# Swin attention before an LIF layer: score products in four 64x64 tiles, q and k moved straight into their stacks

## What is computed

```
part = windows(_gn(x))                       # 8*16 windows, 64 tokens, 256 channels
q, k, v = part @ qkv_w.T + qkv_b             # q scaled by 16 ** -0.5, 16 heads
attn = einsum('wihd,wjhd->whij', q, k) + bias[None, None] + MASK[None, :, None]
attn = softmax(attn, axis=-1)
x = x + einsum('whij,wjhd->wihd', attn, v)
h = einsum('tbld,hd->tblh', _gn(x), W) + b   # then v += (h - v)/2; s = v >= 1; v = v*(1-s)
x = x + spikes
```

## Time and profile before

| | before |
|---|---|
| time, median of 3 runs | 511.57 us (507.66 to 513.79) |
| the profiled execution's own time | 516.01 us |
| its span | 514.3 us |
| granted clock of PE, mean | 0.95 |
| PE, PEld busy | 433.2 us (84%), 400.7 us (78%) |
| DVE, ACT, POOL busy | 408.8 us (79%), 380.1 us (74%), 274.8 us (53%) |
| DMA | 136780 packets, 61.56 MB, of them 107506 under 512 B |

### The profile page before, as it was taken

How to read it: one execution, slowest core, us unless ns; L and a number is a source line. 1 busy time by engine, 2 the same in 40 slices (tenths; PEclk the granted TensorE clock), 3 DMA queues, 4 the chain that set the end, 5 groups by cost and what they waited for, 6 DMA issues and landing times.

```text
span 514.3 us, 19277 instructions
## 1 busy us (share of the span) xinstructions
PE 433.2 (84%) x7848; PEld 400.7 (78%) x7848; DVE 408.8 (79%) x872; ACT 380.1 (74%) x897; POOL 274.8 (53%) x380
## 2 busy tenths in 40 slices
PE   0477956998889879889988898989898987799996
PEld 0366856987889879789878797978798986588885
DVE  7957866798789859868888778879767887588887
ACT  6357776887889869779878787978788957745560
POOL 3534674567566746567666557556756648420000
PEclk9977977999999989989999989999999989889999
DMA  7145551465555563565555555554545450023333
GB/s 216 70 104 144 126 123 47 101 149 134 126 123 136 125 151 83 144 151 130 111 147 127 135 135 132 130 135 104 112 104 116 107 138 13 22 103 124 143 128 139
DMA packets 136780, 61.56 MB, mean 120 GB/s; under 512 B 107506, under 2 KB 125172, under 8 KB 136692
## 3 DMA queue, kind: packets, MB, share of 16 engines
q1 hardware_dynamic: 136352, 60.33, 46.5%
q10 hardware_dynamic: 340, 0.01, 0.0%
HBM read 35.13 MB, written 25.17 MB: 117 GB/s over the span
## 4 chain that ended last, share of the span: by engine, by line
PE 31%; SPq 19%; ACT 13%; DMA 11%; DVE 10%; issue 7%; POOL 7%; ACTq 0%; DVEq 0%; POOLq 0%
SPq L314 13%; DMA k_stack<-k_spill0lo 5%; SPq L309 4%; PE pv_ps L1045 3%; POOL p_lo L446 3%; PE score_ps L923 3%; ACT v_hi L520 3%; PE proj_ps L923 3%; PE pv_ps L923 3%; DMA k_stack<-k_spill1lo 2%; PE proj_ps L934 2%; PE score_ps L1021 2%; ACT k_flat L503 2%; PE max_ps L923 2%; PE proj_ps L935 2%
## 5 line engine op out<-in xcount | busy, mean ns | idle before, releaser
L446 POOL TENSOR_TENSOR p_lo<-probs,p_hi 128x512 f16<-128x512 f32 x128 | 146.4, 1165 | 132.7 <-ACT p_hi L609 78.9
L1011 PE MATMUL score_ps<-q_stack,k_stack 96*128 96x64 f16 x1024 | 86.6, 194 | 45.2 <-ACT max_rows L599 18.0
L1011 PEld LDWEIGHTS score_ps<-q_stack,k_stack 96*128 96x128 f16 x1024 | 71.9, 98 | 52.5 <-ACT max_rows L599 38.5
L608 ACT ACTIVATE probs<-score_ps 128x512 f32<-128x512 f32 x128 | 77.0, 602 | 46.9 <-PE score_ps L1021 43.4
L783 DVE TENSOR_REDUCE neg_max<-max_ps 128x16 f16<-128x1024 f32 x64 | 78.3, 1224 | 27.6 <-PE max_ps L991 26.6
L934 PE MATMUL proj_ps<-xn_hi,w_hi 128*128 128x256 f32 x256 | 78.6, 307 | 12.7 <-DVE w_lo L732 8.1
L1007 PE MATMUL score_ps<-both_parts,bias_k 128*128 128x64 f16 x1024 | 78.3, 194 | 0.0
L609 ACT ACTIVATE p_hi<-score_ps 128x512 f16<-128x512 f32 x128 | 77.4, 605 | 0.0
L777 DVE TENSOR_TENSOR v_lo<-proj_ps,v_hi 64x256 f16<-64x256 f32 x128 | 54.2, 424 | 28.4 <-ACT v_hi L520 26.8
L935 PE MATMUL proj_ps<-xn_lo,w_hi 128*128 128x256 f32 x256 | 74.1, 289 | 0.0
L936 PE MATMUL proj_ps<-xn_hi,w_lo 128*128 128x256 f32 x256 | 73.8, 288 | 0.0
(11 more groups left out here) (130 smaller groups left out, 1214.2 us busy)
## 6 DMA issues: line engine op xcount, KB each, us to landing
xc<-in_x_dram SPq DMA_DIRECT2D x32, 256.0 KB, 3.5
q_spill<-q_flat SPq DMA_DIRECT2D x32, 256.0 KB, 2.7
q_stack<-q_spill SPq DMA_DIRECT2D x32, 256.0 KB, 3.7
out_dram<-xc SPq DMA_DIRECT2D x32, 256.0 KB, 2.3
q_stack<-q_spill SPq DMA_DIRECT2D x32, 128.0 KB, 3.8
k_spill0hi<-k_flat SPq DMA_DIRECT2D x16, 128.0 KB, 2.2
k_spill0lo<-k_flat SPq DMA_DIRECT2D x16, 128.0 KB, 3.3
k_stack<-k_spill0hi SPq DMA_DIRECT2D x32, 64.0 KB, 3.1
```

The costliest lines, as they stand in the source:

```text
L446: pool.tensor_tensor(p_lo[p][:, quads, :, :].rearrange("p g w i -> p (g w i)"), probs[:, quads, :, :].rearrange("p g w i -> p (g w i)"), p ...
L608: act.activation(probs[:, quads, :, :].rearrange("p g w i -> p (g w i)"), score_ps[:, h, :], ACT.Exp)
L1011: pe.matmul(dst, k_stack[slot][0:96, 2 * mid + q, at, :], q_stack[slot][0:96, 2 * mid + q, at, :], start=False, stop=False)
```

## The change

1. `move_q_and_k` no longer goes through DRAM: six calls of `stack` with two DMAs each copy 64 partitions of `q_flat` or `k_flat` straight into 16 partitions of a stack. The stacks hold 48 rows a head: head 0 of each couple from row 0, head 1 from row 64; channels of the second half stand swapped (`r ^ h`). `k_stack` loses its zero blocks and their clearing. The spill semaphores go; `q_high`, `k_high`, `q_low`, `k_low` wait (`await_moved`) until the previous row's whole move has landed.
2. `scores`: 32 q-k products in four 64x64 tiles, then 8 bias products with the biases as moving operand of 512 columns (`bias_s`; `flip` are the weights), then 16 picks. `max_scores`: 4 bias products of 512 columns and 32 q-k products of 64. `turn_maxima`: 4 small products, now at the start of a pair, behind a wait for both exponentials of the pair before.
3. The wait for the next `stacked` stands behind the picks, ahead of `max_scores`.
4. Biases are prepared by 8 instructions of ACT a variant (were 3) and 4 of POOL (was 1). Weights' columns are ordered anew (`w_blocks`), `b_cols` is loaded by 7 DMAs (were 5), and DVE scales the biases ahead of the first norm rather than behind `w_lo`.

```diff
+            def stack(slot, stacks, term, flat, part):
+                for r in range(2):
+                    first = r * WS + term * D
+                    sp.dma_start(stacks[slot][first:first + D, :, :, :].rearrange("d g n i -> d g (n i)"),
+                                 flat[r * WS:(r + 1) * WS, part, :])\
                       .then_inc(stacked[slot], 16)
...
-                sp.wait_ge(k_hi_done, r + 1)
-                spill(k_flat, HI, k_hi_spilled, k_spill[slot][0])
-                sp.wait_ge(k_lo_done, r + 1)
-                spill_q(slot)
+                sp.wait_ge(q_flat_done, r + 1)
                 if not is_first(r, 2):
                     sp.wait_ge(score_ps_done, 4 * (r - 2) + 4)
-                spill(k_flat, LO, k_lo_spilled, k_spill[slot][1])
-                sp.wait_ge(k_hi_spilled, (r + 1) * 16)
-                stack_k(slot, 0, 0, slice(0, QUADS))
...
+                stack(slot, q_stack, 0, q_flat, HI)
+                stack(slot, q_stack, 2, q_flat, HI)
+                sp.wait_ge(k_hi_done, r + 1)
+                stack(slot, k_stack, 0, k_flat, HI)
+                stack(slot, k_stack, 1, k_flat, HI)
+                sp.wait_ge(q_lo_done, r + 1)
+                stack(slot, q_stack, 1, q_flat, LO)
+                sp.wait_ge(k_lo_done, r + 1)
+                stack(slot, k_stack, 2, k_flat, LO)
...
             def q_high(done):
                 act.wait_ge(q_ps_done, done)
-                wait(act, q_spilled, 16 * (done - 1))
+                await_moved(act, done - 1)
...
-            def scores(n, row, k, before_tiles):
+            def scores(n, row, k):
...
+                for g, w in itertools.product(range(QUADS), range(2)):
+                    col = (2 * g + w) * WS
+                    for h, e in itertools.product(range(HALVES), range(2)):
+                        at = h * WCOLS + 2 * p + w
+                        rows = stacks_of[e ^ h]
+                        pe.matmul(score_ps[halves[e], h, col:col + WS], k_stack[slot][rows, g, at, :], q_stack[slot][rows, g, at, :],
+                                  start=(g == 0 and w == 0), stop=False)
...
+                pe.wait_ge(max_rows_done, n + 1)
...
+            dve.wait_ge(b_loaded, 16 * 9)
             dve.tensor_scalar(b_cols[:, 0:HALVES], b_cols[:, 0:HALVES], QK_SCALE, None, ALU.mult)
...
-                scores(n, row, k, await_tile_operands)
+                wait(pe, p_hi_done, n * 2)
+                turn_maxima(n)
+                scores(n, row, k)
...
                 if not is_last_pair(n):
+                    await_max_operands(*following)
                     max_scores(following[2])
```

More of the change, by code:

```diff
@@ L763, in q_low @@
                 dve.wait_ge(q_flat_done, done)
-                wait(dve, q_spilled, 16 * (done - 1))
+                await_moved(dve, done - 1)
                 low_with_bias(q_flat, 0).then_inc(q_lo_done, 1)
@@ L977, in max_scores @@
                 slot = k // 2 % 2
-                halves = [slice(r * WS, (r + 1) * WS) for r in range(2)]
-                for w in range(2):
-                    for mid, rows in enumerate(halves):
-                        for q, queries in enumerate(halves):
-                            pe.matmul(max_ps[queries, mid, w * 256:(w + 1) * 256], ident_h[rows, rows],
-                                      bias_q[rows, variant(k, w), q, :, :].rearrange("p h n -> p (h n)"),
-                                      start=(w == 0), stop=False)
@@ L985, in max_scores @@
-                for w in range(2):
-                    for h in range(HALVES):
-                        col = (2 * w + h) * 128
-                        at = h * WCOLS + 2 * (k % 2) + w
-                        for mid, rows in enumerate(halves):
-                            for q, queries in enumerate(halves):
-                                last = pe.matmul(max_ps[queries, mid, col:col + 128], q_stack[slot][rows, 2 * mid + q, at, :],
-                                                 k_stack[slot][rows, 2 * mid + q, at, :],
-                                                 start=False, stop=(w == 1 and h == 1))
+                first, last_variant = variant(k, 0), variant(k, 1)
@@ new lines, in scores @@
+                first, last_variant = variant(k, 0), variant(k, 1)
+                for part in range(2):
+                    for h, e in itertools.product(range(HALVES), range(2)):
+                        rows = halves[e ^ h]
+                        biases = bias_s[rows, part, first:last_variant + 1, h, :, :].rearrange("p v g i -> p g v i")
+                        if last_variant == first:
+                            biases = biases.to_broadcast([WS, QUADS, 2, WS])
+                        pe.matmul(score_ps[halves[e], h, :].rearrange("p (g w i) -> p g w i", g=QUADS, w=2), flip[rows, :], biases,
+                                  start=False, stop=False)
@@ new lines, in scores @@
+                pe.wait_ge(max_rows_done, n + 1)
+                for w, m in itertools.product(range(2), range(2)):
+                    for h, e in itertools.product(range(HALVES), range(2)):
+                        rows = halves[e ^ h]
+                        dst = score_ps[halves[e], h, :].rearrange("p (m q w i) -> p m w q i", m=2, q=2, w=2)[:, m, w, :, :]
+                        last = pe.matmul(dst, pick_max[rows, (2 * w + m) * 2 + h, :],
+                                         max_rows[p][rows, :].rearrange("p (q i) -> p q i", q=2),
+                                         start=False, stop=(w == 1 and m == 1))
+                        if w == 1 and m == 1 and e == 1:
+                            last.then_inc(score_ps_done, 1)
@@ L1027, in turn_maxima @@
             def turn_maxima(n):
                 pe.wait_ge(neg_max_done, n + 1)
-                pe.transpose(max_ps[:, 0, :].bitcast(f16)[:, 0:128], neg_max[:, :], ident_h[:, :])\
-                  .then_inc(max_turned, 1)
+                for q, queries in enumerate(halves):
+                    for rows in halves:
+                        last = pe.matmul(max_ps[rows, q, 0:WS], neg_max[queries, rows], ident_h[queries, queries], start=True, stop=True)
+                last.then_inc(max_turned, 1)
```

185 lines of the change are left out of this document (76 added, 109 removed).

## The result

| | before | after |
|---|---|---|
| time, median | 511.87 us, 4 runs (507.66 to 513.79) | 562.0 us, 4 runs (561.52 to 565.91) |
| ratio to before, 95% interval | | 1.1009 (1.0924 to 1.1093) |
| span of the profiled execution | 514.3 us | 559.8 us |
| granted clock of PE, mean | 0.950 | 0.905 |
| one row of four windows | 12.35 us | 13.80 us |

What follows compares the result with a forecast made beforehand. ACT was taken to set the row, with the stack wait on top. Terms -19.6 (stack wait), -3.8 (mode change), +3.6 (bias), -3.0 (setup) sum to -22.8 us, from the 511.6 us median to 489 us; range 475 to 503.

Steps and rivals of the forecast that it cites:

- the term of the move: Direct q and k moves into the stacks take 7.9 us, hidden before the next `q_high`; costed at nothing.
- The rival: Late move: at 10.4 us `q_high` waits, closing a loop; row 13.2 us, time 537 us; chance 0.13.
- Stack wait, -19.6: PE's wait for the stack ahead of the last score product, holding ACT's exponentials, goes: -19.6 us.
- Row of 11.6 us: One row of four windows in the attention stretch falls from 12.35 to 11.6 us.
- Score products: In `scores`, 32 small products overlap in four tiles, 0.22 us; all take 0.66 for 1.0, worth nothing.
- Bias, +3.6: Preparing four bias variants on ACT, 8 instructions of 0.40 us each: +3.6 us (+0.8 to +10.8).
- Setup, -3.0: DVE scales biases before the first norm, saving PE's wait before the first v product: -3.0 us.
- Tiles that don't overlap: Rival: a pair's 64 small products take 1.9 instead of 0.44 us; time 537 us; chance 0.04.
- DVE takes the gain back: Rival: DVE, idle only 0.98 us before the reduction, takes half of 23.4 us; time 501 us; chance 0.09.

Runs made afterwards that it cites:

- eight moves: The changed kernel with only 8 of the 12 q and k moves from the third row on (scores wrong by their low parts): 493.81 us, ratio 0.962.
- The new stacks, filled through DRAM: The changed kernel with four writes of the flat parts to DRAM and twelve reads into the stacks, `q_high` etc. waiting only for the writes: 500.68 us.

## Why the prediction was wrong

**The step that failed** is the term of the move: "The whole move then takes 12 x 0.45 + 2.5 = 7.9 us, between 6.6 and 10.4", against a `q_high` that comes 8.8 us after the picks, hence "hidden, with 0.9 us to spare. I cost it at nothing". Measured: 8.79 us of issuing and 1.85 of landing make 10.64, beyond its upper bound, and the first issue comes 0.3 behind the picks; `q_high` came about 11.3 us after them. The landing was put too high by 0.65; the issuing, 5.4 forecast, too low by 3.4. Of that, 12 x (0.594 - 0.45) is 1.7 us, the 0.04 between issues 0.5, and the long issues, 45 in 32 moves with about 0.8 beyond the median each, 1.1.

The trace of before pointed higher. The two q moves in 1.11 us, 0.555 each, went into the stack itself, to 64 and 32 partitions with one run of 4 KB in each, but they were taken as the ceiling. Over the whole trace they are no ceiling: such a move took 0.583 in the median, and one of k's high part 0.553.

```profile
L309 SPq DMA_DIRECT2D q_stack<-q_spill x64: 489/583/1961, 31.5 to 421.9; - x64
L314 SPq DMA_DIRECT2D k_stack<-k_spill0hi x96: 447/553/1810, 28.0 to 409.3; - x96
```

And the six k moves in 4.83 us, 0.8 each, were used only to call the old chain slow; they hold an issue of 2.02 us.

**The rival** had the mechanism, the place and the formula: "the row becomes a loop: move, `q_high` to picks (2.76), move". With 11.3 in place of 10.4 it gives a row of 14.06; 13.80 was measured, since `q_high` to the picks' end took about 2.5. From the forecast's 489 us, 32 x (13.80 - 11.6) = 70 us lead to 559, for 562.0 measured. The 3 us that are left are within the 4.4 us by which the profiled execution of before, which gave the 12.35 and so the 11.6, stood above its median. What was wrong there, beside the move's length, is its chance, 0.13. With a margin of 0.9 us in a term whose bounds span 3.8, and a price of 30 us for each us beyond it, 0.87 for "in time" was too sure.

**The other steps**, which two flat buffers uncover:

- *Stack wait, -19.6.* ACT's wait at the exponentials came out as forecast (20.4 us; "near 33 x 0.6 = 20"). But that is not its worth in time. The wait moved by itself in the kernel before gave 7.5 us (2.7 to 12.2), with ACT's wait for `attn_cm` up by 7.3. The whole change gains 25 us where no engine waits for a stack or a flat buffer any more (487.13).
- *Row of 11.6 us.* 11.81 with two flat buffers, 11.69 with eight moves, 11.53 with two buffers and three slots. Right, had the cover been there: with two flat buffers 32 x 0.21 = 6.7 us of the 9.6 between 489 and 498.57 lie in the rows; the rest stays open.
- *Score products.* 32 small products take 260.83 - 260.57 = 0.26 us (0.22 forecast), at the higher clock, in PE's rows above. That is 8 ns each. By the overhead of each matmul that the Trainium skill gives (TensorEngine Tiling (Array Packing), Instruction Overhead), unshared by tiles, it would have been the prediction's estimated 0.8; the trace stays against that reading.
- *Bias, +3.6.* ACT took 1.44 + 1.45 = 2.89 us a variant for 2.31, 0.36 for each instruction (0.40 forecast): +2.3 us.
- *Setup, -3.0.* The first exponentials come 0.9 us earlier, and that holds two of the four bias variants, which cost 1.2 more than before: about 2.1 for the setup itself. `b_rows` no longer waits (6.71 in the earlier trace rows), and DVE's scaling takes 0.17 us, but the first projections now start later, at 19.08, behind the low part of `xn` on POOL, which begins 0.67 us later and takes 2.35 us instead of 1.40.
- *Tiles that don't overlap; DVE takes the gain back.* Neither: 32 small products behind the picks take 262.59 - 262.24 = 0.35 us or less to the next product, and in the fastest version DVE's reduction waits 9.1 us for the max products, where it waited 26.6 before.

## What to carry over

A wait that is moved from "copied out" to "arrived at the other end" puts the whole transfer, its issuing included, into the loop of the buffer it guards: count the issues, at the median of the nearest moves over the whole trace rather than at one row, and add the long ones. When a cover is as thin as the spread of the term under it, the chance of the loop is not small, and its price counts in every row. The cure was cheap: a second flat buffer, or a semaphore for each part, turned 562 us into 499 and 501, and with a third slot 487.

## What the runs showed of the hardware

**The time to issue a DMA doesn't go by its bytes.** A move of 64 KB from 64 partitions into 16, in runs of 1 KB, takes the SP queue 0.594 us. The same 64 KB into the same 16 partitions, read from DRAM in runs of 4 KB, took 0.42 ("The new stacks, filled through DRAM"). The write of a flat part to DRAM, 128 KB in 128 runs of 1 KB, took 0.34 in the median for k's high part and 0.47 for its low part in the kernel before. Shape is not all of it either. The same load of x, 256 KB to 128 partitions, before and after:

```profile
L347 SPq DMA_DIRECT2D xc<-in_x_dram x24: 431/447/1200, 47.2 to 329.4; - x24
...
L335 SPq DMA_DIRECT2D xc<-in_x_dram x24: 431/583/1627, 42.5 to 360.4; - x24
```

What sets the time no run singles out. The DMA engines are busy 0.24 of the stretch, while SP's queue carries 36% of the chain.

**Long issues coincide with packets of the queue named "instruction".** The page of the kernel after lists the DMA queues (packets, MB, share):

```profile
q1 hardware_dynamic: 41632, 43.55, 23.2%
q8 instruction: 74, 1.21, 0.9%
```

In the trace these 74 packets are of 16 KB and took 1.09 us in the median. All 45 moves whose issue took over 1 us overlap one of them, and of the 339 shorter ones 45 do. In the kernel before, of its reads into the stacks, it is 31 of 31, and 27 of 353. That the fetching of instructions delays the issue is the likely reading; it was only seen, not tried.

**A DVE instruction beside POOL's clearing.** The scaling of a 128x2 tile in the setup took 5.02 us before, from 17.99 to 23.01, while POOL's six clearings ran from 17.26 to 22.98. After, moved ahead of them:

```profile
11.06 0.17 DVE L715 TENSOR_SCALAR b_cols<-b_cols 128x2 f32<-128x2 f32 x1
```

The Trainium skill, SBUF — State Buffer, SBUF: two separate sides, says that a DVE instruction in a mode with two ports and a GpSimd instruction share a pair of ports, which whichever starts first holds for its whole instruction while the other stands still. The times agree with that; whether the scaling ran in such a mode no run shows, and none tried one without the other.
